# A one-core attention, expert and delta-rule kernel: last v lanes loaded by the solve's program, one product ahead of the norms, slots ahead of the tiles' experts, lane-major row sums in DRAM

## The reference

```python
# mixture of experts (layers 2 and 4)
probs = softmax(x @ gate_w);  top_w, top_i = top_k(probs, 2);  top_w /= sum(top_w)
for e in range(8):
    out += route[:, e:e+1] * ((silu(x @ w1[e]) * (x @ w3[e])) @ w2[e])
# delta rule (layer 3)
q = l2norm(conv_silu(silu(x @ Wq.T + bq)));  k = l2norm(...);  v = conv_silu(...)   # l2norm divides by norm + 1e-6
a = sigmoid(x @ Wa.T + ba);  b = sigmoid(x @ Wb.T + bb)
# for each token, for each head:
S = a * S - a * b * (S k) k^T + b * v k^T
o = q S
```

## Time and profile before

| what | value |
|---|---|
| median of the three runs | 1884.42 us |
| the profiled execution: its own time | 1883.49 us |
| span in its trace | 1881.8 us |
| TensorE busy | 1266.9 us (67%) |
| VectorE busy | 1434.8 us (76%) |
| ScalarE busy | 973.7 us (52%) |
| GpSimd busy | 351.4 us (19%) |
| DMA | 92.16 MB in 99034 packets |

### The profile page before, as it was taken

The page is one execution under the profiler, slowest core; times in us unless marked ns, Lnnn a source line. Parts: engine busy times, 40 slices in busy tenths (PEclk is TensorE's granted clock), DMA queues, the critical chain, the costliest instruction groups (busy, mean ns, idle before and its releaser), DMA issues. The chain is left out here.

```text
span 1881.8 us, 42023 instructions
## 1 busy us (share of the span) xinstructions
PE 1266.9 (67%) x15746; PEld 779.3 (41%) x15746; DVE 1434.8 (76%) x2661; ACT 973.7 (52%) x2042; POOL 351.4 (19%) x495
## 2 busy tenths in 40 slices
PE   4689999999999999991599483000000049950998
PEld 2225555555555555451599342000000014430997
DVE  4689999898999989824265485999989979871564
ACT  4638888788888888864266372201222200031564
POOL 6101000000100000005335200000000025536055
PEclk9869999999999999995699785555555569975999
DMA  3521111111111100022312254610221110011222
GB/s 95 172 55 31 31 31 32 31 31 31 31 31 40 40 14 3 3 69 70 77 13 27 54 143 110 179 45 11 68 64 39 40 50 1 1 45 50 53 23 25
DMA packets 99034, 92.16 MB, mean 49 GB/s; under 512 B 21745, under 2 KB 82994, under 8 KB 98450
## 3 DMA queue, kind: packets, MB, share of 16 engines
q1 hardware_dynamic: 83106, 78.18, 16.4%
q0 software_dynamic: 11264, 8.92, 3.3%
q10 hardware_dynamic: 4464, 2.38, 0.5%
HBM read 47.28 MB, written 31.21 MB: 42 GB/s over the span
## 5 line engine op out<-in xcount | busy, mean ns | idle before, releaser
L725 DVE TENSOR_REDUCE att_negmax<-att_ps_max 128x1 f32<-128x1024 f32 x512 | 621.4, 1223 | 74.4 <-PE att_ps_max L595 45.3
L713 ACT ACTIVATE att_probs<-att_ps_prob 128x512 f32<-128x512 f32 x1024 | 556.3, 595 | 135.6 <-PE att_ps_prob L610 132.3
L595 PE MATMUL att_ps_max<-av_k_op,av_q_op 81*32 81x512 bf16 x4096 | 416.5, 394 | 10.9 <-PEq L104 7.2
L610 PE MATMUL att_ps_prob<-av_q_op,av_k_op 99*32 99x512 bf16 x4096 | 410.3, 383 | 2.1 <-DMA av_q_op<-att_nm_parts 0.4
L627 PE MATMUL att_ps_acc<-att_probs,att_vq 128*32 128x256 f32 x4096 | 315.1, 379 | 0.0
L1985 PE MATMUL out_ps_y<-all_bo_row,all_ones 1*128 1x128 f32 x2 | 0.8, 482 | 361.0 <-PEq L104 361.0
L1118 PE MATMUL moe_moe_ps_up<-moe_moe_xgT,moe_moe_wbuf 128*128 x1456 | 196.8, 279 | 0.0
L1118 PEld LDWEIGHTS moe_moe_ps_up<-moe_moe_xgT,moe_moe_wbuf 128*128 128x128 f32 x1456 | 181.4, 196 | 0.1
L595 PEld LDWEIGHTS att_ps_max<-av_k_op,av_q_op 81*32 81x32 bf16 x4096 | 115.5, 97 | 129.6 <-DVE att_negmax L725 28.2
L610 PEld LDWEIGHTS att_ps_prob<-av_q_op,av_k_op 99*32 99x32 bf16 x4096 | 107.7, 95 | 142.0 <-ACT att_probs L713 83.9
L627 PEld LDWEIGHTS att_ps_acc<-att_probs,att_vq 128*32 128x32 f32 x4096 | 133.3, 111 | 77.0 <-issue 0.5
(11 more groups left out here) (278 smaller groups left out, 1768.7 us busy)
## 6 DMA issues: line engine op xcount, KB each, us to landing
av_k_op<-terms_k SPq DMA_DIRECT2D x48, 216.0 KB
av_q_op<-terms_q SPq DMA_DIRECT2D x144, 72.0 KB
solve_dec_and_windows<-solve_Xw SPq DMA_DIRECT2D x16, 256.0 KB, 3.0
solve_dec_and_windows<-b_k_lane SPq DMA_DIRECT2D x16, 256.0 KB, 3.7
moe_moe_xs<-expert_rows SPq DMA_DIRECT2D x6, 576.0 KB, 6.6
terms_q<-qkv_parts_q SPq DMA_DIRECT2D x8, 384.0 KB, 3.1
terms_k<-qkv_parts_k SPq DMA_DIRECT2D x8, 384.0 KB, 3.3
all_w_all<-in_f_w SPq DMA_DIRECT2D x24, 128.0 KB, 2.5
```

What stands on the lines that cost most here:

```text
L595: mm = pe.matmul(ps_max[c * STRIP:(c + 1) * STRIP, n % 2, k * CH:(k + 1) * CH], q_op[s][0:R_ALL, qt // CT, h, at:at + STRIP], k_op[s][0:R_ ...
L610: mm = pe.matmul(ps_prob[c * STRIP:(c + 1) * STRIP, j % 2, :], k_op[s][0:R_END, h, at:at + STRIP], q_op[s][0:R_END, half, h, :], start=Tru ...
L713: act.activation(probs[:, j % PROBS, :], ps_prob[:, j % 2, :], ACT.Exp).then_inc(s_exp, 1)
L725: dve.tensor_reduce(negmax[:, w % 2, a:a + 1], ps_max[:, n % 2, :], AX.X, ALU.max, negate=True).then_inc(s_maxed, 1)
```

## The change

In the mixture of experts: `places` runs ahead of `experts_of_tiles`, and the write that `places` reads is now waited for. In the first of the two layers the DRAM rows of x are ordered by lane (row 32 p + t in place of 128 t + p), and the row numbers with them, so each lane's 32 rows lie together. In the projection: the v lanes of the sequence before are loaded at the beginning of the next sequence's list, ahead of the gates' store; the last sequence's are loaded by SyncE at the beginning of the solve; the projection's block ends with waits for the stores of q and of v. In the solve: the large product of `products(0)` runs before the inversion of the norms.

```diff
@@ moe
-        resid_tiles = resid.rearrange("(t p) c -> p t c", p=P)
+        resid_tiles = resid.rearrange("(p t) c -> p t c" if out is None else "(t p) c -> p t c", p=P)
+        per_tile, per_lane = (1, NT) if out is None else (P, 1)
...
-            pool.iota(xr[:, :, COL_ID:COL_ID + 1].bitcast(mybir.dt.int32), pattern=[[P, NT], [0, 1]], base=0,
-                      channel_multiplier=1).then_inc(s_ids, 1)
+            pool.iota(xr[:, :, COL_ID:COL_ID + 1].bitcast(mybir.dt.int32), pattern=[[per_tile, NT], [0, 1]],
+                      base=0, channel_multiplier=per_lane).then_inc(s_ids, 1)
...
-                also(dve.tensor_tensor(member[:, :, 0:1], base[:, :].unsqueeze(2), before.unsqueeze(2), ALU.add))
+                chain.done(dve.tensor_tensor(member[:, :, 0:1], base[:, :].unsqueeze(2), before.unsqueeze(2), ALU.add))
...
             pair_totals()
+            places()
             experts_of_tiles()
-            places()
             order_passes()
@@ project_conv
             for b in range(B):
+                if b:
+                    load_rows(b - 1, 2, g.v_lane, g.s_vlane)
                 store_gates(b)
                 store_rows(b, 0)
-                if b:
-                    load_rows(b - 1, 2, g.v_lane, g.s_vlane)
                 store_rows(b, 1)
                 load_rows(b, 0, g.k_lane, g.s_klane)
                 store_rows(b, 2)
                 load_gates(b)
-            load_rows(B - 1, 2, g.v_lane, g.s_vlane)
             sp.wait_ge(s_out[1], 16 * B)
+            sp.wait_ge(s_out[2], 16 * B)
@@ solve_and_scan
         def _(sp):
+            for th, lane in lanes_of(B - 1):
+                sp.dma_start(Xv[lane, :, :], of_half(scr.qkv[2], th, B - 1)).then_inc(g.s_vlane, 16)
             sp.wait_ge(s_scaled, 1)
...
         def _(dve):
-            norms = Count(dve, s_inv)
-            dve.wait_ge(s_norm, 1)
-            norms.done(dve.tensor_scalar(norm[:, :, :], norm[:, :, :], L2_EPS, None, ALU.add))
-            norms.done(dve.reciprocal(norm[:, :, :], norm[:, :, :]))
-            dve.tensor_copy(q_scale[:, :], norm[:, 0, :])
-            dve.wait_ge(s_turn, 1)
-            dve.tensor_copy(norm_rows, ps_norm[0:NT, :]).then_inc(s_rows, 1)
...
+            def invert_norms():
+                norms = Count(dve, s_inv)
+                dve.wait_ge(s_norm, 1)
+                norms.done(dve.tensor_scalar(norm[:, :, :], norm[:, :, :], L2_EPS, None, ALU.add))
+                norms.done(dve.reciprocal(norm[:, :, :], norm[:, :, :]))
+                dve.tensor_copy(q_scale[:, :], norm[:, 0, :])
+                dve.wait_ge(s_turn, 1)
+                dve.tensor_copy(norm_rows, ps_norm[0:NT, :]).then_inc(s_rows, 1)
...
-            def products(i):
+            def products(i, between=None):
...
                 chain.done(dve.tensor_tensor(prod.rearrange("p (e c t) -> p e c t", e=D, c=LB), k4[:, :, :, i + 1:],
                                              k4[:, :, :, i:i + 1].to_broadcast(after), ALU.mult))
+                if between:
+                    between()
...
             dve.wait_ge(g.s_klane, 16 * NL)
-            products(0)
+            products(0, invert_norms)
```

## The result

The changed kernel took 1869.89 us (median of five runs, 1865.83 to 1872.48), the kernel before 1884.42 in the same comparison: a ratio of 0.9924, with a 95% interval of 0.9903 to 0.9944. That is 14.5 us less, between 10.6 and 18.3. The sign was right; the size was too small by 5.0 us.

A forecast was written before the change was run, and what follows sets the result against it. It took the scatter, the load of x, SyncE's queue at the projection's end and VectorE in the solve as the path. Terms 1.5 + 1.4 + 5.0 + 1.6 = 9.5 us gave 1874.9 us, range 1870.5 to 1880.0.

The forecast's parts named there:

- slots, two layers: Expert layers' plan: slots ahead of the tiles' experts start the scatters 0.75 us sooner per layer, 1.5 us in all.
- rows of x: Load of x after the first expert layer: 4 KB pieces land sooner and close VectorE's gaps, 1.4 us (0 to 1.7).
- projection's end: Last sequence: v lands sooner and the last v lanes leave the block, 5.0 us (2.6 to 6.7).
- product: Solve's start: the product begins without waiting for the norms, so the sums begin 1.6 us sooner (1.0 to 1.8).
- "at most" of 0.87: Slots: ScalarE's rows end last next, so the gain per expert layer is 0.87 us at most.
- a lone store's 3.0 us: Rows of x: if the first load lands like a 512 KB store in 4 KB pieces, it comes 1.1 us sooner.
- Rivals 2 and 3: DRAM layout of x: brings nothing, 1876.3 us, chance 0.12; or is slow, 1890.3 us, chance 0.03.
- Rival 1: Projection's end: v lands no sooner, only 2.6 us gained there, 1877.3 us in all; chance 0.12.
- the end at which the DMA engines stay the limit: Projection's end: v lands at 1152.0, as 512 KB leave the busy stretch, 2.8 us; the other end was 1148.7.
- the 3.2 foretold: Projection's end: the solve starts about 3.2 us after VectorE's last copy of sums, in place of 8.2.
- the forecast's 1151.0: Projection's end: v lands and the block ends at 1151.0 in place of 1156.01, 5.0 us.

The follow-up runs named there:

- the rows alone: Kernel before with only the DRAM rows of x by lane in the first expert layer: 1880.78 us, ratio 0.9984.
- the lanes alone: Kernel before with only the v lanes' schedule changed, a sequence late and the last ones by the solve: 1879.67 us, ratio 0.998.
- the slots alone: Kernel before with only the slots run ahead of the tiles' experts, in both expert layers: 1877.42 us against 1884.23, ratio 0.996.

## Why the prediction was right in its steps and wrong in its sum

| term | predicted | changed kernel | alone |
|---|---|---|---|
| slots, two layers | 1.5 | 1.85 | 1.85 |
| rows of x | 1.4 | 1.1 | 0.9 |
| projection's end | 5.0 | 4.3 | 4.9 (mean of six against five kernels: 4.65) |
| product | 1.6 | 1.5 | 1.5 |
| the scan's jumps | no term | 4.4 | 4.1 (slots), 4.1 (product) |

**Slots:** right in mechanism, 0.35 us too small. ScalarE ends last, as foretold, and GpSimd's start behind it is 873.23 - 872.35 = 0.88 us. The plan of passes is later and costs nothing. The gains of 0.96 and 0.89 lie 0.09 and 0.02 above my "at most" of 0.87.

**Rows:** the sum nearly right, its make-up not. I had 0.8 to 1.1 us for a first landing that comes sooner and 0.6 for the gaps. The first landing came only 0.2 us sooner, and with the rows alone not at all (4.12 us); over all kernels it took 3.9 to 4.2 us in the new layout and 4.0 to 4.2 in the old. The pace gave the rest: the loads land 1.3 to 1.4 us apart, VectorE's 32 statistics are the slower of the two, and they take 6.29 us in place of 7.18. Taking a lone store's 3.0 us for a load with three others behind it was the fault; what a lone load would take isn't shown. Rivals 2 and 3 fell: the pieces matter, and lanes 16 KB apart run mostly at 410 to 437 GB/s. The rule of the Trainium skill that the prediction weighed ("DMA: Bandwidth & Descriptors", Specifications: line rate from 512 B on) differs from these loads, 285 to 295 GB/s at 512 B and mostly over 400 at 4 KB; the measurement decides.

**The projection's end:** right in mechanism and near in size. Rival 1 (2.6 us only) fell. The k lanes' issue took 1.82 us where under 1.5 was foretold (1.32 with the lanes alone), and v landed 6.2 us after its store's issue, near the end at which the DMA engines stay the limit, as chosen. The solve starts 5.0 us after the end of VectorE's last copy of sums, not the 3.2 foretold. 1.1 us of that is the copy, which itself came earlier, 8.03 us after the gates' store in place of 9.15; in three kernels with the same edits and the copy at 9.15 the solve starts 3.7 to 4.1 us after it. The rest is v: it was stored 1.9 us after the k lanes' issue began, not under 1.5, and landed 6.2 us later, where the forecast's 1151.0 meant 5.4. SyncE's added wait for v, in earlier sequences, pushed no store of the gates back.

**Product:** right: 1.5 us where 1.6 was foretold, and a slack of 1.0 us behind it where 1.1 was.

**The step that failed** is the sum: it has four terms for four edits and takes all other stages as they were, without a word on why, so none for code that only moves. I said of VectorE in the solve that "an idle stretch filled there is also gained whole" but looked for such stretches only ahead of the scan; and I priced the added wait at 0.03 to 0.04 us, not as an instruction that shifts everything behind it. The four terms themselves came to 8.8 us, 0.7 under the forecast and inside its range. The kernel before had its scan at the long place; one added instruction took it off, and 4.4 us went. That they went, and didn't come, is luck: none of the four parts aims at it. The 5.07 us of "issue" at the jump stood in the trace before. Had I asked of every hardware loop behind the edits what it waits for at its jump, and whether its place would change, the term would have been "0 or 4.4", and the range 1866 to 1880.

**What is scatter.** Outside these stages the two traces differ both ways: 2.5 us more ahead of the first expert layer, 1.9 less from the block after the load of x to the last gates' store. The first is no part of the change, which has no line there: over the kernels that layer begins at 851.6 to 854.6 us. Nor is the second: this stretch took 74.1 to 77.1 us over the kernels, with and without each edit. TensorE's granted clock could make it look like the change's, as it stood at 0.50 (the level of 1.2 GHz) from 1132 to 1136 us in the kernel before and at 1.00 (2.4 GHz) from 1130 to 1134 us in the changed one; but the kernels with the slots alone (75.40) and the rows alone (74.16) have the short stretch with no edit to the lanes, the one with the lanes alone the long one (76.92). The parts run alone add up to more than the change, if the jump is counted once: 2.7 + 3.4 + 4.6 + 2.4 + 4.4 = 17.5 us, by the medians. Each has an interval of about 2 us to either side, so this shows no interplay.

**Still open:** where the borders of the fetched blocks lie and whether the long place comes back every 128 or every 256 instructions; why the first load of x takes about 4 us to land in either layout; and why the stretch before the last gates scatters by 3 us.

## What to carry to other kernels

When a change is read, compare the lengths of all stages on both sides, not only of those that it touches: one added instruction moved a later hardware loop and was worth 4.4 us, as much as the largest of the four intended parts. When the trace shows an engine idle with no releaser at the turn of a loop of some hundreds of instructions (420 here), and that engine is the bound, count the instruction packets in the DMA view of that idle time; then write the loop out (6.1 us here), or move it by one wait and measure. And before a small gain is put down to an edit, give the kernel before a wait that does nothing.

## What the runs showed of the hardware that was not expected

- A jump back over 420 VectorE instructions costs 2.7 to 3.0 us of idle time with one fetch of instructions in it. At one place in the list, and again at the place 256 instructions further, it costs 5.0 to 5.5 us, with two fetches at the first jump. Written out, the four bodies run with no wait over 0.3 us in between.
- VectorE's instructions came in packets of 8 KB, one for about 128 instructions (an estimate from 16.3 us between packets and 52.9 us for a body of 420).
- One already met wait on VectorE, ahead of the scan, made the kernel 5.7 us faster (3.4 to 6.8).
- 512 KB loads from DRAM in 512 B pieces run at 285 to 295 GB/s, in 4 KB pieces mostly at 410 to 437. Four in a row land 1.8 to 1.9 and 1.3 to 1.4 us apart, but the first of them takes about 4 us in either case.
